# An 8-bit rounding step built from ScalarE's 8-bit copies instead of float32 additions

## The reference

```
FP8_MAX = 448.0
def _fp8_roundtrip(x):
    return x.astype(jnp.float8_e4m3fn).astype(jnp.float32)
def _div_clamp_fp8(x, scale):
    y = jnp.clip(x.astype(jnp.float32) / scale, -FP8_MAX, FP8_MAX)
    y = y.astype(jnp.bfloat16).astype(jnp.float32)
    return _fp8_roundtrip(y)
```

## Time and profile before

| | |
|---|---|
| median of 3 executions | 2261.65 us (2260.24 to 2263.61) |
| profiled execution, its own time | 2263.61 us |
| its span, first to last instruction | 2262.2 us |
| TensorE matmuls busy | 2000.9 us, 88% |
| VectorE busy | 1108.6 us, 49% |
| ScalarE busy | 966.3 us, 43% |
| GpSimd busy | 500.2 us, 22% |
| mean granted TensorE clock | 0.94 of 2.4 GHz |

### The profile page before, as it was taken

One profiled execution on the slowest core, in us unless ns is written; L12 is line 12 of the kernel. 1 busy time (PEld: TensorE's weight loads), 2 busy tenths in 40 slices (PEclk: granted clock), 3 DMA queues, 4 the chain that ended last, 5 costly groups with the idle time before them and its releaser, 6 DMA issues. The chain is left out here.

```text
span 2262.2 us, 29203 instructions
## 1 busy us (share of the span) xinstructions
PE 2000.9 (88%) x10392; PEld 1665.2 (74%) x10392; DVE 1108.6 (49%) x2434; ACT 966.3 (43%) x1747; POOL 500.2 (22%) x483
## 2 busy tenths in 40 slices
PE   2786859999999999999999999999999994658758
PEld 1455748888888888888888888888888873532546
DVE  4676444354344434434433443443444334978855
ACT  2776234344344434434433443443444323708321
POOL 2553024321111111111111112112112112511321
PEclk9898579999999999999999999999999996979769
DMA  3431264344333424524432442433343215500020
GB/s 127 146 95 37 56 203 131 114 139 134 115 111 114 144 72 139 156 74 128 133 107 87 146 135 88 146 111 112 90 132 120 86 52 197 204 20 3 1 75 19
DMA packets 204438, 243.10 MB, mean 107 GB/s; under 512 B 68224, under 2 KB 126272, under 8 KB 203784
## 3 DMA queue, kind: packets, MB, share of 16 engines
q1 hardware_dynamic: 193800, 240.39, 34.0%
q10 hardware_dynamic: 8448, 0.43, 0.2%
q0 software_dynamic: 2048, 0.43, 0.1%
HBM read 216.06 MB, written 24.58 MB: 106 GB/s over the span
## 5 line engine op out<-in xcount | busy, mean ns | idle before, releaser
L760 PE MATMUL kx_ps<-ctxT_hi,wk_hi 128*128 128x400 f32 (+1 forms) x1024 | 362.5, 354 | 29.2 <-DVE ctxT_lo L881 26.5
L764 PE MATMUL kx_ps<-ctxT_hi,wk_lo 128*128 128x400 f32 (+1 forms) x1024 | 355.1, 347 | 0.0
L762 PE MATMUL kx_ps<-ctxT_lo,wk_hi 128*128 128x400 f32 (+1 forms) x1024 | 355.1, 347 | 0.0
L811 PE MATMUL u_ps<-ctxN_hi,pt_hi 128*128 128x512 f32 (+1 forms) x832 | 344.1, 414 | 3.2 <-DVE pt_lo L915 3.2
L813 PE MATMUL u_ps<-ctxN_hi,pt_lo 128*128 128x512 f32 (+1 forms) x832 | 331.3, 398 | 0.0
L812 PE MATMUL u_ps<-ctxN_lo,pt_hi 128*128 128x512 f32 (+1 forms) x832 | 329.9, 396 | 0.0
L887 DVE TENSOR_TENSOR kx_lo<-kx_ps,kx_hi 128x400 fp32r<-128x400 f32 (+1 forms) x256 | 147.2, 575 | 328.9 <-ACT sq L996 327.2
L915 DVE TENSOR_TENSOR pt_lo<-t_ps,pt_hi 128x512 fp32r<-128x512 f32 (+1 forms) x256 | 145.0, 587 | 300.6 <-ACT pt_hi L1011 300.5
L994 ACT ACTIVATE kx_hi<-kx_ps 128x400 fp32r<-128x400 f32 (+1 forms) x256 | 129.5, 506 | 342.7 <-PE kx_ps L764 341.7
L1091 POOL TENSOR_SCALAR var_col<-ssq_col 128x13 f32<-128x13 f32 x64 | 20.1, 314 | 1130.4 <-DMA ssq_col<-ssq_sb 1130.4
L1011 ACT ACTIVATE pt_hi<-t_ps 128x512 fp32r<-128x512 f32 (+1 forms) x256 | 126.1, 523 | 324.7 <-PE t_ps L798 324.7
(11 more groups left out here) (241 smaller groups left out, 3428.1 us busy)
## 6 DMA issues: line engine op xcount, KB each, us to landing
rstd_bc<-scratch_rstd SPq DMA_DIRECT2D x64, 804.0 KB, 5.1
stage<-in_ctx_t SPq DMA_DIRECT2D x96, 267.0 KB, 3.6
stage<-in_ctx_n SPq DMA_DIRECT2D x96, 256.0 KB, 4.3
wk_hi<-scratch_wk_s SPq DMA_DIRECT2D x56, 256.0 KB, 2.7
wk_lo<-scratch_wk_s SPq DMA_DIRECT2D x56, 256.0 KB, 3.0
wv_hi<-scratch_wv_s SPq DMA_DIRECT2D x56, 256.0 KB, 3.2
wv_lo<-scratch_wv_s SPq DMA_DIRECT2D x56, 256.0 KB, 4.0
cat_raw<-scratch_cat SPq DMA_DIRECT2D x8, 1024.0 KB, 8.0
```

Source lines behind the costliest of these rows:

```text
L760: PE.matmul(kx_ps[:, j % 2, 0:w], wk_hi[:, g % 2, i, :], ctxT_hi[:, i, c0:c0 + w], start=(i == 0), stop=False)
L762: PE.matmul(kx_ps[:, j % 2, 0:w], wk_hi[:, g % 2, i, :], ctxT_lo[:, i, c0:c0 + w], start=False, stop=False)
L764: mm = PE.matmul(kx_ps[:, j % 2, 0:w], wk_lo[:, g % 2, i, :], ctxT_hi[:, i, c0:c0 + w], start=False, stop=(i == C - 1))
L811: PE.matmul(u_ps[:], pt_hi[0:w, t % 2, cols], ctxN_hi[0:w, y, :], start=(y == 0), stop=False)
```

## The change

The clipping moves to VectorE, the rounding to ScalarE's writes of the 8-bit type. With t2 the scaled value clipped to 448 (bf16) and c2 = t2 clipped to 240, ScalarE writes h8 = t2/2, g8 = c2/2 and a8 = c2, each rounded by the write (`d` is bf16; h8, g8, a8 are the 8-bit type; t1 is float32). VectorE then makes d = h8 - g8 and d * 2 + a8: where the value is within 240 d is nil and a8 is the result, above it the halves carry the excess. In the diff the places of use follow the class: VectorE and ScalarE of the first stage, then VectorE and ScalarE of the output projection; of the removed functions only the heads are shown.

```
-    def scalar_scale(self, k, src, recip):
+    def vector_clip(self, k, src, recip):
+        V, s = self.c.DVE, k % self.sets
+        after(V, self.halves, 2 * (k - self.sets + 1))
+        after(V, self.whole, k - self.sets + 1)
+        for c in range(4):
+            V.tensor_scalar(self.t1[:, s, c, :], src[:, c, :], recip[:, c:c + 1], 448.0, ALU.mult,
+                            ALU.min).then_inc(self.scaled, 1)
+        V.wait_ge(self.scaled, 4 * k + 4)
+        V.tensor_scalar(self.t2[:, s, :, :], self.t1[:, s, :, :], -448.0, None, ALU.max).then_inc(self.clipped, 1)
+        V.wait_ge(self.clipped, k + 1)
+        V.tensor_scalar(self.c2[:, s, :, :], self.t2[:, s, :, :], 240.0, -240.0, ALU.min, ALU.max).then_inc(self.inner, 1)
+    def scalar_halves(self, k):
+        A, s = self.c.ACT, k % self.sets
+        A.wait_ge(self.clipped, k + 1)
+        after(A, self.done, k - self.sets + 1)
+        A.activation(self.h8[:, s, :, :], self.t2[:, s, :, :], ACTF.Copy, scale=0.5, saturate=False).then_inc(self.halves, 1)
+        A.wait_ge(self.inner, k + 1)
+        A.activation(self.g8[:, s, :, :], self.c2[:, s, :, :], ACTF.Copy, scale=0.5, saturate=False).then_inc(self.halves, 1)
+    def scalar_whole(self, k):
+        A, s = self.c.ACT, k % self.sets
+        A.activation(self.a8[:, s, :, :], self.c2[:, s, :, :], ACTF.Copy, saturate=False).then_inc(self.whole, 1)
-    def vector_round(self, k, dst):
+    def vector_join(self, k, dst):
         V, s = self.c.DVE, k % self.sets
+        V.wait_ge(self.halves, 2 * k + 2)
+        V.tensor_tensor(self.d[:, s, :, :], self.h8[:, s, :, :], self.g8[:, s, :, :], ALU.subtract).then_inc(self.excess, 1)
+        V.wait_ge(self.whole, k + 1)
+        V.wait_ge(self.excess, k + 1)
+        V.scalar_tensor_tensor(dst[:], self.d[:, s, :, :], 2.0, self.a8[:, s, :, :], ALU.mult, ALU.add).then_inc(self.done, 1)
...
-            quant.vector_round(0, xq[:, 0, :, :])
+            quant.vector_clip(0, lnT, recip[:, 4:8])
+            quant.vector_join(0, xq[:, 0, :, :])
...
+                    if n in first and t == 0:
+                        sc = blocks[n][1]
+                        quant.vector_clip(first[n], lnT, recip[:, 4 * sc:4 * sc + 4])
                     if n in first and t == 3:
...
-                        quant.vector_round(k, xq[:, k % 2, :, :])
+                        quant.vector_join(k, xq[:, k % 2, :, :])
...
                     if n in first and t == 1:
-                        quant.scalar_scale(first[n], lnT, recip[:, 4 * sc:4 * sc + 4])
+                        quant.scalar_halves(first[n])
+                    if n in first and t == 2:
+                        quant.scalar_whole(first[n])
...
+            def clip(n):
+                V.wait_ge(cat_in[n % 2], 16 * (n // 2 + 1))
+                quant.vector_clip(K0 + n, raw[:, n % 2, :, :], recip[:, 4 * n:4 * n + 4])
+            V.wait_ge(scales_set, 2)
+            clip(0)
             for n in range(8):
+                if n + 1 < 8:
+                    clip(n + 1)
                 after(V, part_done, n - 1)
-                quant.vector_round(K0 + n, catq[:, n % 2, :, :])
+                quant.vector_join(K0 + n, catq[:, n % 2, :, :])
...
-            A.wait_ge(scales_set, 2)
             for n in range(8):
-                A.wait_ge(cat_in[n % 2], 16 * (n // 2 + 1))
-                quant.scalar_scale(K0 + n, raw[:, n % 2, :, :], recip[:, 4 * n:4 * n + 4])
                 A.wait_ge(w_in[n % 2], 16 * (n // 2 + 1))
                 after(A, part_done, n - 1)
                 A.activation(w_hi[:, n % 2, :, :], w_raw[:, n % 2, :, :], ACTF.Copy).then_inc(high_done, 1)
+                quant.scalar_halves(K0 + n)
+                quant.scalar_whole(K0 + n)
```

More of the change, by code:

```diff
@@ L167, in __init__ @@
         self.c = core
-        self.scaled, self.clipped, self.grid_set = core.sem("q_scaled"), core.sem("q_clipped"), core.sem("q_grid")
-        self.sized, self.lifted, self.done = core.sem("q_sized"), core.sem("q_lifted"), core.sem("quantized")
+        self.scaled, self.clipped, self.inner = core.sem("q_scaled"), core.sem("q_clipped"), core.sem("q_inner")
+        self.halves, self.whole, self.excess = core.sem("q_halves"), core.sem("q_whole"), core.sem("q_excess")
+        self.done = core.sem("quantized")
@@ L171, in place @@
     def place(self, stack, tag, sets):
         core, self.sets = self.c, sets
[L173 to L177, removed]
-    def scalar_scale(self, k, src, recip):
-        A, s = self.c.ACT, k % self.sets
[L181 to L186, removed]
@@ L188, in vector_round @@
-    def vector_round(self, k, dst):
-        V, s = self.c.DVE, k % self.sets
[L190 to L200, removed]
+        self.t1 = core.sb(stack, f"t1_{tag}", [P, sets, 4, 512])
@@ new lines, in place @@
+        self.t2 = core.sb(stack, f"t2_{tag}", [P, sets, 4, 512], BF16)
+        self.c2 = core.sb(stack, f"c2_{tag}", [P, sets, 4, 512], BF16)
+        self.a8 = core.sb(stack, f"a8_{tag}", [P, sets, 4, 512], FP8)
+        self.h8 = core.sb(stack, f"h8_{tag}", [P, sets, 4, 512], FP8)
+        self.g8 = core.sb(stack, f"g8_{tag}", [P, sets, 4, 512], FP8)
+        self.d = core.sb(stack, f"d_{tag}", [P, sets, 4, 512], BF16)
+    def vector_clip(self, k, src, recip):
[9 more added lines that the diff above has]
+        V.tensor_scalar(self.c2[:, s, :, :], self.t2[:, s, :, :], 240.0, -240.0, ALU.min, ALU.max).then_inc(self.inner, 1)
@@ L479, in scalar @@
             A.wait_ge(scales_set, 5)
-            A.wait_ge(feat.moved, 4)
-            quant.scalar_scale(0, lnT, recip[:, 4:8])
+            quant.scalar_halves(0)
+            quant.scalar_whole(0)
             for c in range(3):
@@ L501, in scalar @@
                     if n in first and t == 1:
-                        sc = blocks[n][1]
-                        quant.scalar_scale(first[n], lnT, recip[:, 4 * sc:4 * sc + 4])
+                        quant.scalar_halves(first[n])
+                    if n in first and t == 2:
+                        quant.scalar_whole(first[n])
                 if 7 <= i <= 19 and i % 4 == 3:
```

## The result

The changed kernel took 2287.58 us (median of 4 executions, 2283.02 to 2292.95) and the kernel before, on the same chip, 2260.94 us (4 executions, 2255.02 to 2263.61): a ratio of 1.0122 with a 95% interval of 1.0092 to 1.0152. It is slower, by 26.6 us of the medians; 24.5 had been forecast, and a median of 2286.2 us. The profiled execution took 2284.88 us with a span of 2283.5 us.

A forecast was written before the change was run, and what follows sets the result against it. VectorE, taking turns with GpSimd's wp_lo, was taken to bound the projection, and a chain through VectorE and ScalarE the first stage. 11.0 + 13.5 = 24.5 us gave 2288.1 for the profiled execution, median 2286.2, range 2275 to 2295.

The forecast's parts named there:

- +11.0 forecast: First stage: the quantisations k = 0 to 3 lose 1.1, 4.7, 2.6 and 2.6 us, in sum 11.0 us.
- the clip part: VectorE's share of one quantisation: four float32 clips 2.0 us, clip to bf16 1.25, bf16 clip 0.68, together 3.95 us.
- Rival E: First stage: the clip is absorbed and only ScalarE's extra 1.15 us counts, +5 instead of +11 us, total 2280; chance 0.15.
- Rival C: TensorE falls to its lower clock in longer waits; the first stage would pay 1 to 4 us, total 2289; chance 0.20.
- +13.5 forecast: Output projection: the last join ends at 2003.2 us against 1989.7, with VectorE's steps 12.95 us instead of 10.3.
- stretched by GpSimd: Output projection: VectorE and GpSimd's wp_lo take turns, which adds 4.35 us to each of eight steps.
- That leaves room: Output projection: ScalarE's copies, done 15.5 us after join n, and wp_lo leave room for the 8.3 us of sums.
- The 16.9: Output projection: join n+2 starts 12.95 + 3.95 = 16.9 us after join n.
- behind that end come 17.7 us of VectorE work that the change doesn't touch: End of the output projection: 17.7 us of VectorE work follow the last catq's end, unaffected by the change.
- A: VectorE's subtraction runs at two columns a cycle, 1.23 us, about 9 us less, total 2277; chance 0.10.
- B: ScalarE's 8-bit writes take double, 3.8 us, in both stages, 34 us more, total 2320; chance 0.04.
- D: The two joins run at 1.23 us each without excluding GpSimd; projection 10 us sooner, total 2259; chance 0.03.

## Why the prediction was right

The forecast median was 2286.2 us, the measured one 2287.58. The mechanism is the one forecast, but both of the signs that the prediction had named for being wrong are there as well: steps under 12 us (8.2 and 8.9), and ScalarE as what the join waits for. What that means is told under the projection.

**First stage, +11.0 forecast, +9.6 measured** (+9.4 between the means of five traces with the old and seven with the new first stage, the one with the moved clip left out; the old ones spread over 4.4 us, the new ones over 2.6). Summed up to the row products of k = 1, and to xq of k = 2 and 3, I had 5.8, 8.4 and 11.0 us, and measured 4.9, 6.7 and 8.8. Each step was 0.4 to 0.8 us smaller than priced; 0.35 of it is the clip part, which takes 3.6 us instead of 3.95. The join's second half waits for ScalarE's third copy, as said (0.88 us). Rival E (+5) fell: the clip isn't absorbed. Rival C's clock effect is there (the row products take 2.77 instead of 1.88 us, their granted clock falls to 0.50 on the way and was 1.00 before) but is within these numbers.

**Projection, +13.5 forecast, +16.6 measured.** The mechanism holds: VectorE sets the stage, and wp_lo is worked off in turn with its operations, the 8-bit ones included. The Trainium skill (SBUF — State Buffer, "SBUF: two separate sides") has it so for any operation with two SBUF inputs, and this trace agrees both ways: the wp_lo of 1944.48 takes 6.34 us behind a join with an 8-bit input, and the 8-bit subtractions of 1940.86 and 1990.28 take 3.15 and 3.63 us instead of 2.28 while a wp_lo ends. The terms, though, went both ways:

| us | forecast | measured |
|---|---|---|
| stage start to first clip | 8.4 | 8.2 |
| VectorE's own eight steps | 68.8 | 65.4 |
| stretched by GpSimd | 34.8 | 27.0 |
| VectorE's waits between first clip and last join | 0.7 | 9.1 |
| wait for the total behind the last join | 0 | 5.55 |

Measured are 8 x 8.17 us (1.68 + 1.23 + 0.69 + 2.28 + 2.29); the groups' busy sum of 92.4 us less that; 7.4 us for g_c and 1.7 for a tile. The first four give 109.7 us; the last join ends 110.1 us after the start of the stage (2005.19), the rest being small gaps, against 112.7 forecast.

Two steps of the argument failed. The first is "That leaves room" for ScalarE. It set ScalarE's halves, ready 13.7 us after join n (8.2 for TensorE's step, 5.5 for three operations of ScalarE), against a join n+2 that VectorE reaches 16.9 us after join n. Neither number held:

- The halves were ready 16.1 us after join 0 and 14.6 after join 4. TensorE began these steps at half its clock, and ScalarE's wp_hi could start 10.5 and 9.1 us after the join. This makes 3.3 us of waiting.
- VectorE was ready after 11.8 us both times (1924.71 to 1936.47, and 1975.55 to 1987.30). The 16.9 counted one stretched operation in every step, but wp_lo of step n+2 waits for the same wp_hi as the halves do, and so ran only when VectorE was idle or about to be (1937.24 and 1986.66). With the halves ready at 13.7 us there would still have been 1.9 and 2.0 us of waiting (an estimate from these times).

Together these are nearly the 7.4 us of waits for g_c. That wp_lo ran mostly inside them, and stretched the subtractions behind by 0.9 and 1.35 us instead of 4.3, is most of why "stretched by GpSimd" fell by 7.8 us: the two entries of the table belong together.

The second is "behind that end come 17.7 us of VectorE work that the change doesn't touch". It overlooked that the total's product is queued on TensorE behind step 6, and starts 9.8 us behind the end of step 6's catq in the kernel before and 9.9 us behind it in the changed one. Before, all of VectorE's step 7 stood behind that catq, with its y stretched to 4.97 us: 10.3 us, just enough. The new order has the clip of step 7 ahead of it, and wp_lo stretches catq of step 6 itself (6.52 us), so only the join of 4.65 us is left behind it. That is the 5.55 us, of which moving the total gave back 4.4. The old rounding shows the same wait as soon as GpSimd holds nothing up: 3.0 us where the low part is left out, 2.4 where VectorE makes it.

That the sum came out within 3.1 us of the forecast in this stage, and the median within 1.4 us, is luck: cheaper clips and less stretching (-11.2 us) met waits of +14, and the first stage was 1.4 us cheaper.

**Rivals.** A (1.23 us) fell in the size, 2.28; but the reason I gave against it, "two inputs", was wrong: two bf16 inputs with a bf16 output take 1.22 us, the 8-bit inputs make it 2.28. B fell, a copy to 8 bits takes 1.89 us. D fell: a join part is 4.6 us and holds GpSimd up. C is half right: the low clock is there, but it costs little by TensorE's own steps; it costs through ScalarE's wait for them (3.3 us of the 7.4) and in part through the late total.

## What to carry to other kernels

When an operation is issued earlier, look at what used to be hidden in the stretch that disappears: here a small product behind 32 others had been on time only because VectorE still had a whole step of its own to do and was held up in it for 4.3 us. When a second engine shares the bottleneck engine's access, ask whether the bottleneck could do the work itself: here 18 us of its own work instead of 27 us held up, and with the shorter waits 16.7 us of the stage. When a price is added to every step, look at what the operation that causes it waits for: here it waited for the same thing as the bottleneck, so it fell into some steps and not into others. And when a gain in one stage doesn't reach the end, follow the new wait to its own cause; a transfer queued behind one that nobody needs yet looks like a slow engine.

## What the runs showed of the hardware

- VectorE, 128x2048: a subtraction of two 8-bit tiles to bf16 takes 2.28 us, of two bf16 tiles 1.22 us; the fused form of a bf16 and an 8-bit tile to 32 bits 2.29 us.
- ScalarE writes 128x2048 of the 8-bit type in 1.89 us, as long as bf16 or 32 bits.
- VectorE's two operations with 8-bit inputs and GpSimd's subtraction exclude each other like 16- and 32-bit operations (wp_lo 6.34 us instead of 4.5 behind the fused form; the 8-bit subtraction 3.15 and 3.63 us instead of 2.28 behind wp_lo).
- In the changed kernel's projection TensorE comes back from waits of 4.07, 8.79 and 9.10 us at a granted clock of 0.50 (first product 0.80 us) and goes to 1.00 after about 4.8, 5.3 and 2.9 us, in that order; after a wait of 2.67 us it starts at 1.00 (first product 0.50 us). The wait's length alone doesn't decide: with the bf16 subtraction it started at 0.50 after 2.28 us and with a first product of 0.50 us after 3.92.
- The same code of the cross attention takes 1589.4 to 1595.8 us in different executions, 0.4%. What makes the difference stays open; a change of a few us can only be read in its own stage.
